# Second row scores moved behind the values, a bias row's butterfly moved from VectorE to GpSimd, and more filler matmuls at the start of the last attention

## The reference

```python
x = x + tanh(g_xattn[i]) * attention_i(layernorm(x), ctx)
x = x + tanh(g_ffn[i])   * ffn_i(layernorm(x))
```

## Time and profile before

| | us |
|---|---|
| median of 3 runs | 2375.6 (2373.09 to 2390.44) |
| the profiled execution | 2380.77 |
| its span, first to last instruction | 2379.0 |
| narrow attention of layer 0 | 14.8 to 394.4 |
| wide attention of layer 1 | 462.3 to 1063.2 |
| wide attention of layer 2 | 1230.2 to 1776.2 |
| narrow attention of layer 3 | 1923.7 to 2216.0 |

### The profile page before, as it was taken

One profiled execution on the slowest core, in us unless ns is written; L12 is line 12 of the kernel. 1 busy time (PEld: TensorE's weight loads), 2 busy tenths in 40 slices (PEclk: granted clock), 3 DMA queues, 4 the chain that ended last, 5 costly groups with the idle time before them and its releaser, 6 DMA issues. The chain is left out here.

```text
span 2379.0 us, 42737 instructions
## 1 busy us (share of the span) xinstructions
PE 2002.6 (84%) x16853; PEld 1147.1 (48%) x16853; DVE 1312.5 (55%) x2340; ACT 981.5 (41%) x1888; POOL 864.9 (36%) x1162
## 2 busy tenths in 40 slices
PE   6888897769999999976949999999978969999535
PEld 2333334435555555554734556565555523444423
DVE  4899894145555555524436555555522255887381
ACT  2444453215454444433524544444432214666201
POOL 2466620005555555533024665555530010110024
PEclk9887897959999999997978999999985875999657
DMA  6201100210000000003120000000000021220202
GB/s 225 91 29 45 36 17 1 51 30 5 5 5 4 5 1 2 1 18 123 30 73 5 5 5 5 5 1 2 1 13 0 1 62 34 57 55 17 75 13 24
DMA packets 78710, 69.97 MB, mean 29 GB/s; under 512 B 11744, under 2 KB 68209, under 8 KB 78485
## 3 DMA queue, kind: packets, MB, share of 16 engines
q1 hardware_dynamic: 71789, 53.12, 8.0%
q10 hardware_dynamic: 2888, 9.97, 1.1%
q0 software_dynamic: 3840, 4.20, 0.9%
HBM read 50.47 MB, written 17.31 MB: 28 GB/s over the span
## 5 line engine op out<-in xcount | busy, mean ns | idle before, releaser
L762 POOL TENSOR_TENSOR L1x_fold<-L1x_probs 128x512 f32<-128x512 f32 x128 | 162.4, 1269 | 202.9 <-ACT L1x_probs L830 197.3
L762 POOL TENSOR_TENSOR L2x_fold<-L2x_probs 128x512 f32<-128x512 f32 x128 | 162.4, 1269 | 184.0 <-ACT L2x_probs L830 178.6
L355 ACT ACTIVATE L0x_probs<-L0x_st_ps 128x512 f32<-128x512 f32 x256 | 139.1, 595 | 162.5 <-PE L0x_st_ps L428 145.7
L1134 DVE TENSOR_REDUCE L2x_neg_max<-L2x_row_ps 128x2 f32<-128x1024 f32 x128 | 156.4, 1222 | 81.2 <-PE L2x_row_ps L958 81.2
L1134 DVE TENSOR_REDUCE L1x_neg_max<-L1x_row_ps 128x2 f32<-128x1016 f32 x128 | 155.3, 1213 | 80.9 <-PE L1x_row_ps L958 80.9
L830 ACT ACTIVATE L1x_probs<-L1x_st_ps 128x512 f32<-128x512 f32 x256 | 138.9, 594 | 134.5 <-PE L1x_st_ps L972 133.6
L830 ACT ACTIVATE L2x_probs<-L2x_st_ps 128x512 f32<-128x512 f32 x256 | 138.9, 594 | 129.0 <-PE L2x_st_ps L972 129.0
L544 DVE TENSOR_REDUCE L3x_neg_max<-L3x_row_ps 128x2 f32<-128x1024 f32 x128 | 156.2, 1223 | 47.4 <-PE L3x_row_ps L417 45.8
L355 ACT ACTIVATE L3x_probs<-L3x_st_ps 128x512 f32<-128x512 f32 x256 | 139.1, 595 | 89.8 <-PE L3x_st_ps L428 89.6
L544 DVE TENSOR_REDUCE L0x_neg_max<-L0x_row_ps 128x2 f32<-128x1024 f32 x128 | 155.0, 1214 | 13.4 <-PE L0x_row_ps L417 12.4
L990 PE MATMUL L1x_u_ps<-L1x_probs,L1x_vst 128*64 128x256 f32 x1024 | 127.0, 391 | 1.2 <-ACT L1x_probs L830 1.2
(11 more groups left out here) (589 smaller groups left out, 4924.8 us busy)
## 6 DMA issues: line engine op xcount, KB each, us to landing
L0w_up<-in_L_ffn_up_weights ACTq DMA_DIRECT2D x9, 512.0 KB
L0w_down<-in_L_ffn_down_weights ACTq DMA_DIRECT2D x9, 512.0 KB
L0x_kst<-scratch_L0x_k SPq DMA_DIRECT2D x8, 512.0 KB, 4.1
L3x_kst<-scratch_L3x_k SPq DMA_DIRECT2D x8, 512.0 KB, 4.2
scratch_L0x_k<-L0x_k_hi SPq DMA_DIRECT2D x16, 128.0 KB, 2.3
L0x_qst<-scratch_L0x_q SPq DMA_DIRECT2D x8, 256.0 KB, 2.8
scratch_L3x_k<-L3x_k_hi SPq DMA_DIRECT2D x16, 128.0 KB, 2.3
L3x_qst<-scratch_L3x_q SPq DMA_DIRECT2D x8, 256.0 KB, 2.8
```

What stands on the lines that cost most here:

```text
L355: act.activation(probs[n % PROBS][:, 2 * half:2 * half + 2, :], st_ps[half][:, :, :], ACT.Exp, scale=sh.scale).then_inc(exp_ready, 1)
L762: pool.tensor_tensor(fold[:, :, :], pr[:, 0:2, :], pr[:, 2:4, :], ALU.add).then_inc(fold_step, 1)
L1134: dve.tensor_reduce(neg_max[k % 4][:, t, r % 2, :], row_ps[:, :, 0:sh.keys], AXX, ALU.max, negate=True)\
```

## The change

Three edits, none of which changes what is computed.

1. In both wide attentions PE's order becomes: middle uses, `values(n - 1)`, `row_scores(r, 1)`. DVE's order becomes: first maximum, middle uses, second maximum, end uses.
2. The 54 operations on the bias row move from DVE to POOL, behind the 108 operations on the matrices, and POOL takes two operations a step (one where n is divisible by 3) instead of one (two where n is divisible by 3).
3. The narrow attention has a separate number of filler matmuls, `lead_fill`, for steps before n = 4 (`HG` = 4). It is 2 in layer 0, which is what it was, and 3 in layer 3, where it was 1.

```diff
                 if folding and n >= HEADS:
-                    for _ in range(2 if n % 3 == 0 else 1):
+                    for _ in range(1 if n % 3 == 0 else 2):
                         if folded < folding.matrix_ops:
                             folding.matrix_op(pool, folded)
                             folded += 1
+                        elif rows_done < folding.row_ops:
+                            folding.row_op(pool, rows_done)
+                            rows_done += 1
...
-                keep_busy(n + LEAD, sh.step_fill if n < STEPS else 0)
+                keep_busy(n + LEAD, sh.lead_fill if n < HG else sh.step_fill if n < STEPS else 0)
...
-                if folding and n >= HEADS and rows_done < folding.row_ops:
-                    folding.row_op(dve, rows_done)
-                    rows_done += 1
...
                 for key in sh.mid_uses(n):
                     use(key)
+                if 0 <= n - 1 < LAST_PAIR:
+                    values(n - 1)
                 if 0 <= r < LAST_PAIR:
                     row_scores(r, 1)
-                if 0 <= n - 1 < LAST_PAIR:
-                    values(n - 1)
...
                     row_max(r, 0)
+                for key in sh.mid_uses(n):
+                    take(key)
+                if 0 <= r < LAST_PAIR:
                     row_max(r, 1)
-                for key in sh.mid_uses(n) + sh.end_uses(n):
+                for key in sh.end_uses(n):
                     take(key)
...
-                                             opening_fill=(24, 6), step_fill=2),
+                                             opening_fill=(24, 6), lead_fill=2, step_fill=2),
...
-                                         opening_fill=(24, 6), step_fill=1),
+                                         opening_fill=(24, 6), lead_fill=3, step_fill=1),
```

More of the change, by code:

```diff
@@ L86, with __init__ @@
 class Narrow:
-    def __init__(self, name, clip, bias, mask, out_bias, gate, opening_fill, step_fill):
-        self.opening_fill, self.step_fill = opening_fill, step_fill
+    def __init__(self, name, clip, bias, mask, out_bias, gate, opening_fill, lead_fill, step_fill):
+        self.opening_fill, self.lead_fill, self.step_fill = opening_fill, lead_fill, step_fill
         self.name, self.clip, self.bias, self.mask, self.out_bias, self.gate = name, clip, bias, mask, out_bias, gate
@@ L274, in split_max @@
                 pool.tensor_tensor(second, kept, first, ALU.subtract).then_inc(parts_ready, 1)
-            folded = 0
+            folded = rows_done = 0
             for v in vst:
@@ L305, in _ @@
                             folded += 1
+                        elif rows_done < folding.row_ops:
+                            folding.row_op(pool, rows_done)
+                            rows_done += 1
             if folding:
-                assert folded == folding.matrix_ops
+                assert folded == folding.matrix_ops and rows_done == folding.row_ops
         @block.scalar
@@ L536, in _ @@
                     take(key)
-            rows_done = 0
             for n in sh.steps():
@@ L553, in _ @@
                        .then_inc(capped_dve, 1)
-                if folding and n >= HEADS and rows_done < folding.row_ops:
-                    folding.row_op(dve, rows_done)
-                    rows_done += 1
-            if folding:
-                assert rows_done == folding.row_ops
 PAIRS = HEADS // 2
@@ L1474, in matrix_op, with row_op @@
             self.part(pool, self.matrix_step, self.w_exp[:, :], self.t, self.up[:, n, :], n, False, which, 2 * k)
-    def row_op(self, dve, k):
+    def row_op(self, pool, k):
         n, which = divmod(k, 6)
         if (n, which) == (0, 0):
-            dve.wait_ge(self.loaded, 16 * (6 + 2 * self.stages))
-        self.part(dve, self.row_step, self.b_exp[:, :], self.t_row, self.up[0:1, n, :], n, False, which, 2 * n)
+            pool.wait_ge(self.loaded, 16 * (6 + 2 * self.stages))
+        self.part(pool, self.row_step, self.b_exp[:, :], self.t_row, self.up[0:1, n, :], n, False, which, 2 * n)
 def butterfly_ffn(nc, name, x_res, gates, const, ready):
```

## The result

The changed kernel takes 2268.4 us (median of 4 runs, 2255.81 to 2280.10), the kernel before beside it 2374.8: a ratio of 0.9548, 95% interval 0.9509 to 0.9588. That is 106 us less, twice the 53 forecast and outside the range. A second set of six runs gave 2278.3 us and 0.9586 (0.9543 to 0.9630): 95 us. The profiled execution of the first set was the fastest of its four (2255.81 us, span 2254.0), so I give the profiled one of the second (span 2278.2) beside it wherever they differ. A stage here runs from its first instruction to that of the next.

What follows compares the result with a forecast made beforehand. The prediction saw the wide attentions bound by PE's work and stalls, L0x by PE and DVE waiting in turns, L3x by PE. Edits 1 to 3: -38 + 3 - 18 = -53 us from 2375.6, so 2322 us, range 2308 to 2336.

Steps and rivals of the forecast that it cites:

- Rival 3: In L0x, the bias row hides in POOL's idle time, so 23 us are not lost: 2299 us; chance 0.12.
- Rival 4: In L0x, POOL's two operations a step hold up its splits, 0.8 instead of 0.43 us each: +20, 2342 us; chance 0.10.
- rival 2: Wide attentions: second maximum too late for the next row scores, up to 1.20 us in 59 odd steps: 2393 us; chance 0.06.
- K to values: Wide attentions: PE's change from K's last matmul to the values, unknown between 0 and 0.10 us, taken as 0.10.
- The other bound for the changes: Wide attentions: PE's new order saves 19 us on changes between matmul kinds, instead of the 9 us used.
- The 2 us lost in the two leads: L1x and L2x, steps -4 to -1: `k_lo` directly before the second maximum costs 2 us, bounds 0 to 5.
- rival 1: In L3x, the clock falls anyway despite the added fillers: gain 2 instead of 18 us, 2338 us; chance 0.12.
- The 2 us that I gave back for the first batch: In L3x, the first batch has no output work of an earlier one, which gives back some 2 us.

## Why the prediction was wrong

**Edit 2 is the step that failed.** It said "the stage pays (47.8 - 42.0)/16 = 0.36 us for each" on DVE and "0.43 us each" on POOL, a net of 3 us lost. The runs have 36.7/54 = 0.68 us on DVE beside the matrices, and 5 to 13 us for the 54 on POOL, 0.1 to 0.24 each: a net of 24 to 32 us gained. Both slopes came from windows that differ in more than the folding. The 47.8 stands at clock 0.79 and the 42.0, with matrices only, at 0.92; the steps of the 42.0 (78 to 93) take 42.4 us at 0.88 in the kernel without rows and 35.7 at 1.00 without any folding. The 32.9 lies in the last batches, where there are no projections: the same steps 98 to 113 take 32.8 without any folding, middle ones 35.7. Steps 38 to 53, the place of the 47.8, take 37.7 in the kernel without rows, at 1.00. So an operation of the matrices costs (37.7 - 35.7)/21.3 = 0.09 us there, not 0.43, and one of the row (47.8 - 37.7)/16 = 0.63, of which some 0.48 would stay at clock 1.00. The first error halved the gain, the second made up the loss. Rival 3, the row hides on POOL, was nearly the right mechanism with a chance of 0.12, and its sign, 40 us or less for 16 steps, came (39.0, 38.3); but it too took the 0.36 for the gain. Rival 4 fell: from 130 to 290 us POOL still waits at 12 of some 16 splits for DVE's maximum, so it isn't late with these:

```profile
POOL L0x_shift_parts L268 <- DVE L0x_neg_max L546: 29.4, 12, 5.2
```

"GPSIMD Engine Reference" of the Trainium skill, section When to use GPSIMD, spoke against the edit. The single operation is slower there, as the page has it, but by less than its factor of about 2: a product of the row takes 0.83 to 0.87 us on POOL while DVE is idle or takes a maximum (5 of the 36) and 0.61 on DVE, 1.4 times; the mean in the loop is 1029 ns. That didn't decide, because POOL had idle time (busy 30.84 of 47.80 us in the earlier trace rows) and DVE little (43.63).

**Edit 1: right mechanism, too small.** Forecast 38 us, measured 52 to 58 in the profiles. All that was named came: the waits for the maximum gone, no new one (rival 2 fell), K to values at 0.31 us. (The other bound for the changes, 19 us, should have been 2 x 59 x 7/8 x 0.19 = 19.6; nothing hangs on it.) Steady batches were forecast at 62.0 and 60.7 and are 61.6 and 60.2. The stalls were undersized, and that is the term of the sum that fell short: the waits view counts the time in which the records of PE show nothing, and a matmul's record (0.39 us) is longer than the 0.21 until the next may start. Start to start, the stalls of a steady batch are 2.9 us in L1x and 2.0 in L2x, not 2.7 and 1.5; with 0.65 from the changes of kind that gives 3.6 and 2.6, where 3.6 and 2.7 were measured. Over 12 steady batches that is 5 us. The first batches gained 5.2 and 4.0 us instead of 3.3 and 2.2, in part at a low clock. And the last steps, from step 56 to the end of the stage, gained 6.4 and 5.2 us (L1x, L2x), 4.1 in each in the second profile. I had counted half a batch there, 1.6 and 1.1, and 1.19 us for the longest stall. But the kernel before has one of 1.9 us among these steps in each layer (PE waits for L1134 until 1003.2 and until 1718.4 us), and it is gone. The clock rose there too, from 0.93 to 1.00 and from 0.91 to 0.98; how the rest divides stays open. The 2 us lost in the two leads were 1.1, and 2.0 in the second profile.

**Edit 3: right, a little small.** Forecast 18, measured 22. The clock was 1.00 through the first steps; rival 1 fell. Steps -6 to 21 took 43.4 us, not 50: I had given the 22 steps from 0 on the pace of a steady batch (1.81 us each), but steps 6 to 21 took 26.6 us, 1.66 each, and those before them ran at the pace of the lead, 16.8 us for 12. The 2 us that I gave back for the first batch were too few.

**The sum.** L0x explains 27 to 35 us of the miss, edit 1 15 to 20, edit 3 4; in the first set untouched code adds 13 that the second hasn't.

## What to carry to other kernels

Before a slope is read off two windows, check that they differ in the one thing only: clock and the other uses of the loop must be the same, or a window from the same place in a loop without the work must be found. Work on an engine with little idle time left can cost the loop most of its length, more if a neighbour slows it, and more again if the clock is lower in the slower loop; the same work can nearly vanish on the neighbour, or later on the same engine. And a stall read as idle time between matmuls is a lower bound; count it from start to start.

## What the runs showed of the hardware

DVE and POOL slow one another. In L0x of the changed kernel the clip, the same operation each time, takes 0.68 us beside a small operation of the split (POOL L268, 8 elements a partition) and 0.95 or 1.06 beside a product:

```profile
201.45 0.68 DVE L554 TENSOR_SCALAR L0x_probs<-L0x_probs 128x1024 f32<-128x1024 f32 x1
...
202.71 2.99 POOL L1454 TENSOR_TENSOR L0w_t<-L0w_w_conT,L0w_down 128x256 f32<-128x256 f32 x3
...
203.19 0.95 DVE L554 TENSOR_SCALAR L0x_probs<-L0x_probs 128x1024 f32<-128x1024 f32 x1
...
205.19 1.06 DVE L554 TENSOR_SCALAR L0x_probs<-L0x_probs 128x1024 f32<-128x1024 f32 x1
```

Over that stage the 33 clips that meet nothing on POOL average 684 ns, the 39 that meet only operations on the matrices 992, and the 21 that meet only row operations, on one partition, 964; the longest is 1486. The other way round, a product of the matrices takes 878 ns on average when DVE is only taking a maximum beside it (10 of them) and 1140 when a clip comes in as well (40). "SBUF — State Buffer" of the Trainium skill, section Who interferes with whom, names a port pair that the two share and lock for a whole instruction. These rows agree with a shared resource, and the 0.80 us that the longest clip loses are about a whole product without a clip beside it; they don't prove the lock.

One filler a step fewer brought the clock of L0x down to 0.62, from 0.96 and 0.93 in the two profiles of the changed kernel, and made the stage 94 and 86 us longer. L3x with one filler a step in its lead fell to the low level in all ten traces. It came back after 24 us in two of them and after 61 to 65 in the eight others, with nothing in the stage's code to tell them apart.
